# Metaformer kernel on one core: products stored by image, half of the masks on GpSimd, and the front in smaller pieces

## The chip, the core and the metric

The kernel runs on one core of a Trainium2 chip. The metric is the device time of one execution in microseconds, as the median of several runs. TensorE (PE) multiplies and transposes, VectorE (DVE) and ScalarE (ACT) read what it leaves in PSUM, GpSimd (POOL) works between buffers in SBUF, and SyncE (SP) issues most DMAs. Each engine goes through its own instructions in order and waits for the others by semaphores.

## What is computed

A block of four parts, each a norm and a mixing step with a residual: a spectral convolution, experts, a swept convolution, experts.

```python
# x (8, 32, 64, 64); _ln_c: mean and variance over the 32 channels of a pixel
def _L0_conv_ref(x, w1_real, w1_imag, w2_real, w2_imag):
    xf = jnp.fft.rfft2(x, norm='forward')
    top = jnp.einsum('bixy,ioxy->boxy', xf[:, :, :32, :32], w1)
    bot = jnp.einsum('bixy,ioxy->boxy', xf[:, :, -32:, :32], w2)
    ...
    return jnp.fft.irfft2(out_fft, s=(h, w), norm='forward')

def _L0_ffn_ref(x, gate_w, gate_b, weight1, weight2):      # L1 the same
    logits = jnp.einsum('bsd,ed->bse', x, gate_w) + gate_b  # 16 experts
    probs = jax.nn.softmax(logits, axis=1)                  # over the 4096 tokens
    vals, idx = jax.lax.top_k(probs.transpose(0, 2, 1), K)  # K = 8
    ...
    pooled = jnp.einsum('bked,bke->bed', gathered, topv)
    h = jax.nn.gelu(jnp.einsum('ebd,edh->ebh', h, weight1), approximate=False)
    out = jnp.einsum('ebh,eho->ebo', h, weight2)
    weighted = jnp.einsum('beo,bke->bkeo', out, topv)
    return outputs.at[arange(B)[:, None], flat_idx].add(weighted)

# L1_conv: four sweeps (down, up, right, left); each row is
#   row + relu(conv1d of the row before, 9 taps)

x = x + _L0_conv_ref(_ln_c(x), ...)
t = _to_tokens(x); t = t + _L0_ffn_ref(_ln_t(t), ...)
x = _from_tokens(t, x); x = x + _L1_conv_ref(_ln_c(x), ...)
t = _to_tokens(x); t = t + _L1_ffn_ref(_ln_t(t), ...)
```

## The kernel before

The whole problem stays in SBUF: RA, RB, RC and RD (the last two together RCD) hold 128 x 8192 floats each, RE the spectral weights and scratch. Partitions are four images times 32 channels, or, after a transposition, pixels. PS is PSUM, eight banks of 512 floats. There is no scheduler: each engine's program is written out by hand, and the order on an engine is that of the code.

**First norm** (`norm_tokens(0)`, L477, L801, L999): x comes in eight pieces of 1,024 columns on SP's queue, the six tables `dft` in one load on ACT's. TensorE first runs 42 multiplications of nothing (`keep_warm`), then `centre_group(g)` (L459) subtracts the channel mean of group g into a PSUM slot of two banks; ACT squares it (L809), VectorE sums (L966), ACT takes the root (L791), VectorE the reciprocal (L973) and scales (L976), TensorE applies the transform along a row as the `follower` (L496), ACT drains it into RC (L798). There are four slots, so group g+4 is centred once group g's follower is drained. VectorE takes total(g+1) ahead of norm(g).

**Spectrum** (from L501): `turn_rows_of_spectrum(j)` transposes a group (L430), ACT or VectorE drains it into RA, `spectrum(c)` (L537) transforms along the columns for chunk c of eight, `spread` (L1041, L840) copies the result into the block form XB in eight pieces each on VectorE and ACT, and `mix(c)` (L557) multiplies by the weights, 64 matmuls that the profile counts as 128, in four parts k of a bank each. VectorE drains parts 0 and 1 into Z, ACT parts 2 and 3. Groups 4 to 7 are turned at the head of mix(0) to mix(3). The weights of chunk c (2 MB, `wspec`) go into one of three places; chunks 3 to 7 are asked for by SP when mix(c-3), the last user of the place, is done (L360). Ahead of mix(0) stand the two projections of the gates and 14 idle multiplications.

**Back** (L572 to L641): the products are transposed (two times eight groups), ACT copies the imaginary part to `imtmp` (L856), VectorE combines both into V (L1062, L1063), chunk by chunk. V lies in RA as (chunk, x, a, re/im, y and image), so that the 128 numbers that `turn_spectrum` (L596, L430) takes for one image stand eight floats apart. ACT drains (L861), `dft_h` (L603) and `dft_w_back` (L633) invert the transform, with transpositions between them.

**Experts** (`experts(l)`): logits by token, the eight largest of each row by `max`, and `match_replace` (L1119) into L2 with the eight replaced by -3e38, while ACT forms all exponentials E (L885). `mask(g)` (L1126) on VectorE keeps E where L2 was replaced, for four quarters g. TensorE turns quarter g (L430), 14 idle multiplications follow for g < 2, VectorE scales (`weigh`, L1132), and `pool_tokens` (L686) sums. `rs_row` and `rs_rep` carry the reciprocal of the softmax's sum by ACT, TensorE (L702) and ACT. In the second layer VectorE takes the four masks in a row, in the first the last two stand between the weighings.

The swept convolution (L753 to L779 and its partners) is not touched.

## Time and profile before

| what | us |
|---|---|
| median of 3 runs | 574.76 (574.59 to 575.63) |
| the profiled execution | 575.6 |
| its span | 573.8 |
| TensorE busy | 533.4 |
| VectorE, ACT, GpSimd busy | 333.3, 296.9, 63.6 |
| granted clock, mean | 0.976 |

The span is what the trace covers; 1.8 us of the profiled execution lie around it. The trace gives for each engine when an instruction started, how long it took and what ended its wait. Neighbouring instructions of one line are merged into one row with a count. TensorE's matmuls overlap, so that the row of a group is more telling than the time of one.

### The profile page before, as it was taken

What the parts mean: (1) busy time and instruction counts of PE and PEld (TensorE: products, weight loads), DVE (VectorE), ACT (ScalarE), POOL (GpSimd) and SP (SyncE); (2) the same over time, 40 slices, a digit from 0 to 9 for tenths busy, and PEclk for the clock granted to TensorE, in tenths of its full rate; (3) what the DMA queues carried; (4) which work ended last, traced back from release to release, by engine and by line L of the source; (5) the groups of instructions that cost most, each with busy time, mean ns of one, the idle gap of its engine ahead of it and who ended that gap; (6) DMA issues with size and microseconds to landing.
All of it is one profiled execution on the core that took longest, in us unless ns stands there. A gap on an engine that the chain in (4) does not pass through costs nothing.

```text
span 573.8 us, 26756 instructions
## 1 busy us (share of the span) xinstructions
PE 533.4 (93%) x11432; PEld 494.5 (86%) x11432; DVE 333.3 (58%) x826; ACT 296.9 (52%) x762; POOL 63.6 (11%) x62
## 2 busy tenths in 40 slices
PE   8889899899997999899999999989999999977895
PEld 8889899899996895689999999989999999976782
DVE  2767686635459926874445444434544455389826
ACT  4556575732278502465555555576666555567300
POOL 4000000020021000000000033320000044640000
PEclk9999999999999888999999999999999999999978
DMA  9941782330000000000000024330000244410007
GB/s 353 376 149 55 270 336 83 137 159 2 1 2 0 2 22 0 2 1 3 2 0 0 4 61 103 76 39 3 0 0 2 47 76 70 78 29 1 2 3 292
DMA packets 48159, 40.80 MB, mean 71 GB/s; under 512 B 42554, under 2 KB 42810, under 8 KB 46877
## 3 DMA queue, kind: packets, MB, share of 16 engines
q1 hardware_dynamic: 46606, 37.27, 20.2%
q0 software_dynamic: 1344, 2.17, 1.8%
q8 instruction: 55, 0.90, 0.6%
q10 hardware_dynamic: 144, 0.39, 0.2%
q14 instruction: 10, 0.07, 0.0%
HBM read 27.49 MB, written 4.19 MB: 55 GB/s over the span
## 4 chain that ended last, share of the span: by engine, by line
PE 70%; DVE 18%; ACT 3%; SPq 2%; POOL 2%; issue 2%; DMA 1%; DVEq 0%; ACTq 0%
PE PS L769 34%; PE PS L557 6%; PE PS L469 4%; PE PS L430 4%; PE PS L603 3%; PE PS L686 3%; PE PS L633 3%; PE PS L762 3%; DVE sums L1084 2%; PE PS L537 2%; DVE RCD L1096 2%; PE PS L463 2%; PE PS L496 2%; DVE sums L966 2%; SPq L332 2%
## 5 line engine op out<-in xcount | busy, mean ns | idle before, releaser
L769 PE MATMUL PS<-RE,conv_sb 128*64 128x64 f32 x6048 | 228.7, 227 | 2.5 <-DVE RE L1198 2.0
L769 PEld LDWEIGHTS PS<-RE,conv_sb 128*64 128x64 f32 x6048 | 211.0, 137 | 11.7 <-DVE RE L1198 4.4
L1198 DVE SCALAR_TENSOR_TENSOR RE<-PS,RE 128x64 f32<-128x64 f32 x504 | 113.1, 225 | 120.9 <-PE PS L769 110.3
L762 PE MATMUL PS<-ones_bf,biasT 128*64 128x64 bf16 x1008 | 100.5, 192 | 0.5 <-DVE RE L1191 0.4
L902 ACT ACTIVATE RE<-RCD 128x128 f32 (+1 forms) x126 | 38.9, 310 | 52.1 <-DVE RE L1198 52.0
L762 PEld LDWEIGHTS PS<-ones_bf,biasT 128*64 128x64 bf16 x1008 | 60.0, 112 | 1.5 <-ACT RCD L798 0.5
L469 PE MATMUL PS<-warm 128*128 128x128 bf16 x524 | 39.1, 241 | 4.0 <-DVE ones_bf L961 1.5
L469 PEld LDWEIGHTS PS<-warm 128*128 128x128 bf16 x524 | 35.3, 109 | 5.4 <-ACT RB L882 1.6
L321 POOL DMA_DIRECT2D RE<-RCD x32 | 18.6, 588 | 181.7 <-ACT RCD L905 181.7
L902 ACT ACTIVATE RE<-RE 128x128 f32 (+1 forms) x63 | 26.6, 422 | 19.5 <-DVE RE L1198 17.2
L905 ACT COPY RB<-RE 128x128 f32 (+1 forms) x126 | 35.6, 283 | 1.5 <-DVE RE L1198 1.5
L557 PE MATMUL PS<-RE,RB 128*64 128x64 f32 x1024 | 32.4, 223 | 3.2 <-issue 3.2
L905 ACT COPY RCD<-RE 128x128 f32 (+1 forms) x122 | 34.4, 282 | 0.7 <-DVE RE L1198 0.7
L557 PEld LDWEIGHTS PS<-RE,RB 128*64 128x64 f32 x1024 | 31.0, 138 | 4.2 <-issue 3.6
L902 ACT ACTIVATE RE<-RB 128x128 f32 (+1 forms) x63 | 19.5, 310 | 25.2 <-DVE RE L1198 25.1
L966 DVE TENSOR_REDUCE sums<-RE 128x32 f32<-128x1024 f32 x16 | 19.4, 1217 | 20.0 <-ACT RE L809 20.0
L1041 DVE COPY RB<-PS 32x256 f32<-32x256 f32 x64 | 26.7, 417 | 7.2 <-PE PS L537 6.5
L861 ACT COPY RB<-PS 128x512 f32<-128x512 f32 (+1 forms) x24 | 16.2, 735 | 26.9 <-PE PS L430 26.9
L1084 DVE TENSOR_REDUCE sums<-RE 128x32 f32<-128x1024 f32 x16 | 19.4, 1212 | 16.4 <-ACT RE L873 9.4
L809 ACT ACTIVATE RE<-PS 128x1024 f32<-128x1024 f32 x16 | 16.2, 1020 | 24.4 <-PE PS L463 21.3
L339 POOL TENSOR_TENSOR RA<-RCD 128x1024 f32<-128x1024 f32 x6 | 17.2, 2894 | 103.9 <-DMA RCD<-RB 103.9
L840 ACT COPY RB<-PS 32x256 f32<-32x256 f32 x64 | 24.1, 377 | 8.4 <-PE PS L537 7.7
(120 smaller groups left out, 753.0 us busy)
## 6 DMA issues: line engine op xcount, KB each, us to landing
RE<-wspec SPq DMA_DIRECT2D x8, 2048.0 KB, 9.0
RA<-x_in SPq DMA_DIRECT2D x8, 512.0 KB, 7.4
RCD<-x_in SPq DMA_DIRECT2D x1, 4096.0 KB, 13.2
out<-RA SPq DMA_DIRECT2D x8, 512.0 KB, 3.5
RCD<-RB SPq DMA_DIRECT2D x48, 64.0 KB, 2.1
RCD<-RB SPq DMA_DIRECT2D x26, 32.0 KB, 1.9
conv_sb<-conv_w SPq DMA_DIRECT2D x1, 768.0 KB, 20.0
RE<-RCD SPq DMA_DIRECT2D x8, 96.0 KB, 4.1
```

The source lines that it names most:

```text
L430: m = pe.transpose(out, lhs[own], ident[own, own])
L469: pe.matmul(PS[:, bank, 0:P], warm[:, :], warm[:, :], start=True, stop=True)
L557: m = pe.matmul(o[:, x % 2, y], XB[:, c % 2, x, 2 * y + a].rearrange("p r q b -> p (r q b)"), WR[:, c % 3, a, x, y, :], start=True, stop=True)
L762: pe.matmul(conv_bank(u, h)[MO * o:MO * (o + 1)], biasT[:, s, MO * o:MO * (o + 1)], ones_bf[:, :], start=True, stop=False)
L769: m = pe.matmul(conv_bank(u, h)[MO * o:MO * (o + 1)], conv_sb[:, s, d, MO * o:MO * (o + 1)], prev, start=False, stop=(d == 2))
L840: m = act.copy(o, i)
L902: act.activation(rowb[:, u], row_at(SRC[s], s, q, u), ACT.Identity).then_inc(s_row, 1)
L905: act.copy(row_at(DST[s], s, q, u), state[:, state_slot(s, u), :, 1:1 + HO]).then_inc(s_arc, 1)
L966: dve.tensor_reduce(sums[:, 32 * g:32 * g + 32], square[:, g % 2, 0:1024].rearrange("p (a c) -> p a c", c=C), AX_X, ALU.add).then_inc(s_su ...
L1041: m = dve.tensor_copy(o, i)
L1084: dve.tensor_reduce(sums[:, 32 * g:32 * g + 32], square[:, g % 2, 0:1024].rearrange("p (a c) -> p a c", c=C), AX_X, ALU.add).then_inc(s_su ...
L1198: dve.scalar_tensor_tensor(out=state[:, state_slot(s, u), k, 1:1 + HO], in0=conv_bank(u, h), scalar=0.0, in1=rowb[:, u, k], op0=ALU.max, o ...
```

## The change

Four things change.

1. *Front.* Piece 0 of x is loaded in two halves. ACT's queue loads the centring table alone, the other five come on SP's queue behind piece 1. 24 idle multiplications stand first, where 42 stood. ACT's first activation is a Sqrt of one column.
2. *Norm's tail and first chunk.* Group 0 is turned ahead of follower(6). The drain of the last follower and that of turned group 2 are cut in two, half on ACT and half on VectorE. spread(0) runs in two halves of eight copies each per engine; mix(0) starts its parts 0 and 1 on the first half and turns group 4 between parts 1 and 2.
3. *Products by image.* V is stored as (chunk, re/im, image, y, q), `imtmp` in the same order, and the table `inv_h` is permuted to fit. ACT and VectorE now read PSUM with eight floats between neighbours and write in a row, and TensorE reads the 128 numbers of an image in a row.
4. *Masks.* Quarters 2 and 3 are formed otherwise: ACT takes Exp of L2 in place (zero where replaced) ahead of `rs_row`, and GpSimd subtracts that from E.

```diff
 @block.sync
-            for g in range(8):
+            sp.dma_start(RA[:, 0:BANK], x_in[:, 0:BANK]).then_inc(s_x[0], 16)
+            sp.dma_start(RA[:, BANK:2 * BANK], x_in[:, BANK:2 * BANK]).then_inc(s_xh, 16)
+            for g in range(1, 8):
                 sp.dma_start(RA[:, 1024 * g:1024 * g + 1024], ...).then_inc(s_x[g], 16)
+                if g == 1:
+                    sp.dma_start(dft_sb[:, 1:6, :], dft[:, 1:6, :]).then_inc(s_dft, 16)
 @block.gpsimd
+            def masks(l):
+                for g in (2, 3):
+                    pool.wait_ge(s_exl, 2 * l + g - 1)
+                    chosen = CW[l][:, 1024 * g:1024 * g + 1024]
+                    pool.tensor_tensor(run_rows(chosen) if l else chosen, part(E, l, g), part(L2, l, g),
+                                       ALU.subtract).then_inc(s_mskp, 1)
...
             pool.memset(state, 0.0).then_inc(s_pad, 1)
+            masks(0)
...
             squares(1)
+            masks(1)
 @block.tensor
                 for n in range(8):                     # centre_group(0, g)
+                        if g == 0 and n == Q:
+                            pe.wait_ge(s_xh, 16)
...
+                    if ln == 0 and g == 6:             # norm_tokens
+                        pe.wait_ge(s_fd, 5)
+                        turn_rows_of_spectrum(0)
                     follower(g)
...
-            keep_warm(7, 42)
-            pe.wait_ge(s_dft, 16)
+            keep_warm(7, 24)
+            pe.wait_ge(s_ctr, 16)
             def dft_w(g):
+                if g == 0:
+                    pe.wait_ge(s_dft, 16)
...
-            pe.wait_ge(s_fd, 5)
-            turn_rows_of_spectrum(0)
             pe.wait_ge(s_fd, 6)
             turn_rows_of_spectrum(1)
             pe.wait_ge(s_fd, 8)
+            pe.wait_ge(s_fdd, 1)
             turn_rows_of_spectrum(2)
             turn_rows_of_spectrum(3)
...
                     wait_rows_turned(pe, 2)            # spectrum(0)
+                    pe.wait_ge(s_t2d, 1)
...
             def mix(c):
-                pe.wait_ge(s_xbd, c + 1)
-                pe.wait_ge(s_xba, c + 1)
-                if c < 4:
-                    turn_rows_of_spectrum(4 + c)
+                if c == 0:
+                    pe.wait_ge(s_mixh, 1)
+                    pe.wait_ge(s_mixd, 1)
+                else:                                  # as before
...
-                    elif k >= 2:
+                    elif k == 2:
+                        pe.wait_ge(s_xbd, 1)
+                        pe.wait_ge(s_xba, 1)
+                        turn_rows_of_spectrum(4)
                         pe.wait_ge(s_gpc, 1)
...
-                turn(c, [V_of_b[:, c, :, BH * bl + bh] for bh in range(BH) for bl in range(BL)])
+                turn(c, [V_of_b[:, c, BH * bl + bh] for bh in range(BH) for bl in range(BL)])
...
-                    pe.wait_ge(s_msk, 4 * l + g + 1)
+                    if g < 2:
+                        pe.wait_ge(s_msk, 2 * l + g + 1)
+                    else:
+                        pe.wait_ge(s_mskp, 2 * l + g - 1)
 @block.scalar
-            act.dma_start(dft_sb[:], dft).then_inc(s_dft, 16)
+            act.dma_start(centre, dft[:, 0, :]).then_inc(s_ctr, 16)
...
+                        if ln == 0 and g == 7:         # drain_follower
+                            o, i = o[..., 0:8], i[..., 0:8]
...
             act.wait_ge(s_set, N_SET)
+            act.activation(std[:, 255:256], eps_sb[:, 0:1], ACT.Sqrt, bias=eps_sb[:, 0:1], scale=1.0 / C)
             norm_tokens(0, f1_pairs)
-            drain(2, t1_pairs)
+            act.wait_ge(s_full, 3)
+            for o, i in t1_pairs(2):
+                act.copy(o[:, :, 0], i[:, :, 0]).then_inc(s_da, 1)
...
-                for o, i in xb_pairs(c, 2):            # spread(c); the same on VectorE
+                if c == 0:
+                    for o, i in xb_pairs(c, 2, 0, X8 // 2):
+                        m = act.copy(o, i)
+                    m.then_inc(s_mixh, 1)
+                for o, i in xb_pairs(c, 2, 0 if c else X8 // 2):
...
-                act.copy(imtmp[:, c % 2, :], banks(4 * (c % 2) + 2, 2)).then_inc(s_tmp, 1)
+                im = banks(4 * (c % 2) + 2, 2).rearrange("p (y r q b) -> p r b y q", r=2, q=Q, b=B)
+                act.copy(im_of(c), im).then_inc(s_tmp, 1)
...
+                act.wait_ge(s_rep, l + 1)
+                for g in (2, 3):
+                    left = part(L2, l, g)
+                    act.activation(left, left, ACT.Exp, bias=negmax[:, :]).then_inc(s_exl, 1)
                 act.wait_ge(s_rt, l + 1)
 @block.vector
-            for j in (0, 1, 3):
-                drain(j, t1_pairs)
+            drain(0, t1_pairs)
+            dve.wait_ge(s_ff, 8)
+            for o, i in f1_pairs(7, ln_slot(7)):
+                dve.tensor_copy(o[..., 8:16], i[..., 8:16]).then_inc(s_fdd, 1)
+            drain(1, t1_pairs)
+            dve.wait_ge(s_full, 3)
+            for o, i in t1_pairs(2):
+                dve.tensor_copy(o[:, :, 1], i[:, :, 1]).then_inc(s_t2d, 1)
+            drain(3, t1_pairs)
...
-                by_re = banks(4 * (c % 2), 2).rearrange("p (a x r n) -> p x a r n", x=X8, a=2, r=2)
-                by_im = imtmp[:, c % 2, :].rearrange("p (a x r n) -> p x a r n", x=X8, a=2, r=2)
+                by_re = banks(4 * (c % 2), 2).rearrange("p (y r q b) -> p r b y q", r=2, q=Q, b=B)
+                by_im = im_of(c)
...
-                mask(0)
-                mask(1)
-                if l == 1:
-                    mask(2)
-                    mask(3)
+                for g in range(2):
+                    mask(dve, l, g, s_msk)
                 weigh(0)
-                if l == 0:
-                    mask(2)
                 weigh(1)
-                if l == 0:
-                    mask(3)
                 weigh(2)
                 weigh(3)
```

The line numbers of the changed program differ: L489 is the centring (L459 before), L536 the follower (L496), L458 the transposition (L430), L499 the idle multiplication (L469), L572 the spectrum (L537), L599 the products (L557), L552 the gates (L518). TensorE from the centring of group 7 to mix(0), before:

```order
10 L459 MATMUL PS<-dft_sb,RA 128x128 x8
11 L496 MATMUL PS<-dft_sb,RCD 128x128 x24
12 L430 MATMUL PS<-dft_sb,RCD 128x64 x64
13 L469 MATMUL PS<-warm 128x128 x16
14 L537 MATMUL PS<-dft_sb,RA 128x128 x16
15 L518 MATMUL PS<-gate_sb,dft_sb 128x64 x2
16 L469 MATMUL PS<-warm 128x128 x14
17 L430 MATMUL PS<-dft_sb,RCD 128x64 x16
18 L557 MATMUL PS<-RE,RB 64x2x32 x64
```

The same stretch of TensorE in the changed program:

```order
10 L489 MATMUL PS<-dft_sb,RA 128x128 x8
11 L536 MATMUL PS<-dft_sb,RCD 128x128 x8
12 L458 MATMUL PS<-dft_sb,RCD 128x64 x16
13 L536 MATMUL PS<-dft_sb,RCD 128x128 x16
14 L458 MATMUL PS<-dft_sb,RCD 128x64 x48
15 L499 MATMUL PS<-warm 128x128 x16
16 L572 MATMUL PS<-dft_sb,RA 128x128 x16
17 L552 MATMUL PS<-gate_sb,dft_sb 128x64 x2
18 L499 MATMUL PS<-warm 128x128 x14
19 L599 MATMUL PS<-RE,RB 64x2x32 x32
20 L458 MATMUL PS<-dft_sb,RCD 128x64 x16
21 L599 MATMUL PS<-RE,RB 64x2x32 x32
```

Sixteen transpositions (group 0) moved ahead of the last two followers, and group 4's moved into the middle of mix(0).

VectorE in the first expert layer, from the replacement on, before:

```order
94 L1119 MATCH_REPLACE RCD<-top,RB 128x4096
95 L1121 RECIPROCAL rsum<-expsum 128x1
96 L1126 SCALAR_TENSOR_TENSOR RCD<-RCD 128x1024 x2
97 L1132 TENSOR_TENSOR RE<-PS,rstd 128x1024
98 L1126 SCALAR_TENSOR_TENSOR RCD<-RCD 128x1024
99 L1132 TENSOR_TENSOR RE<-PS,rstd 128x1024
100 L1126 SCALAR_TENSOR_TENSOR RCD<-RCD 128x1024
101 L1132 TENSOR_TENSOR RE<-PS,rstd 128x1024 x2
```

VectorE there in the changed program, the same rows up to the pooled sums:

```order
99 L1188 MATCH_REPLACE RCD<-top,RB 128x4096
100 L1190 RECIPROCAL rsum<-expsum 128x1
101 L354 SCALAR_TENSOR_TENSOR RCD<-RCD 128x1024 x2
102 L1194 TENSOR_TENSOR RE<-PS,rstd 128x1024 x4
103 L1211 TENSOR_TENSOR pooled<-PS,rs_rep 32x16 x8
```

Two masks are left on VectorE, with the four weighings behind them; the second layer reads the same (it had four masks in a row, then four weighings).

ACT in the second expert layer, from the loading of the exponential's table on, before:

```order
266 L885 ACT_TABLE_LOAD
267 L885 ACTIVATE RCD,expsum<-RCD,negmax 128x4096
268 L887 COPY rs_row<-PS 1x128
269 L889 COPY rs_rep<-PS 32x128
270 L891 ACT_TABLE_LOAD
```

ACT there in the changed program:

```order
269 L940 ACT_TABLE_LOAD
270 L940 ACTIVATE RCD,expsum<-RCD,negmax 128x4096
271 L944 ACTIVATE RCD<-RCD,negmax 128x64x16 x2
272 L946 COPY rs_row<-PS 1x128
273 L948 COPY rs_rep<-PS 32x128
274 L950 ACT_TABLE_LOAD
```

Two exponentials of a quarter stand between the large one and the copy of the row `rs_row`; GpSimd has two subtractions of 128x1024 per layer, the last of its work in the second.

## Rows read from the trace of the kernel before

**Rows 1.** The page: engines, busy us (share of the span) xinstructions.

```profile
PE 533.4 (93%) x11432; PEld 494.5 (86%) x11432; DVE 333.3 (58%) x826; ACT 296.9 (52%) x762; POOL 63.6 (11%) x62
```

**Rows 2.** Timeline 0 to 18: start us, us, engine, line, operation, xcount [idle before <-releaser].

```profile
1.52 4.66 PE L469 MATMUL PS<-warm 128*128 128x128 bf16 x42 [1.52 <-DVE ones_bf L961]
...
5.97 7.83 PE L459 MATMUL PS<-dft_sb,RA 128*128 128x128 f32 x64
...
8.53 1.28 ACT L809 ACT_TABLE_LOAD   x1 [8.53 <-PE PS L459]
...
11.78 1.28 ACT L791 ACT_TABLE_LOAD   x1
...
13.82 1.23 DVE L976 TENSOR_TENSOR RCD<-PS,rstd 128x1024 f32<-128x1024 f32 x1
```

**Rows 3.** Stretches: us, busy (and count) of PE, PEld, DVE, ACT, POOL; clock, DMA.

```profile
6.00:7.00 1.00, 1.00 (x7) 1.00 (x6) 0.00 (x0) 0.00 (x0) 1.00 (x1) 1.00 1.02 418
7.00:8.00 1.00, 1.00 (x11) 1.00 (x11) 0.00 (x0) 0.00 (x0) 0.66 (x1) 1.00 1.00 406
```

**Rows 4.** Timeline, TensorE at the end of the first norm.

```profile
36.77 3.84 PE L496 MATMUL PS<-dft_sb,RCD 128*128 128x128 f32 x32 [1.52 <-DVE RCD L976]
```

**Rows 5.** Timeline, spread(0), idle multiplications, the gate copy, first products.

```profile
45.81 3.07 ACT L840 COPY RB<-PS 32x256 f32<-32x256 f32 x8 [2.33 <-PE PS L537]
45.81 3.43 DVE L1041 COPY RB<-PS 32x256 f32<-32x256 f32 x8 [1.03 <-PE PS L537]
...
47.79 0.94 PE L469 MATMUL PS<-warm 128*128 128x128 bf16 x14
...
49.27 0.29 DVE L1046 COPY proj<-PS 128x128 f32<-128x128 f32 x1
...
49.94 3.95 PE L557 MATMUL PS<-RE,RB 128*64 128x64 f32 x128
```

**Rows 6.** Timeline: a weights' load issued, and TensorE's pauses without a releaser.

```profile
53.93 15.86 SPq L360 DMA_DIRECT2D RE<-wspec  x3
...
62.58 0.33 PE L557 MATMUL PS<-RE,RB 128*64 128x64 f32 x2 [2.19 <-issue]
...
81.92 2.05 PE L537 MATMUL PS<-dft_sb,RA 128*128 128x128 f32 x16
...
91.39 7.51 PE L557 MATMUL PS<-RE,RB 128*64 128x64 f32 x250 [0.65 <-issue]
```

**Rows 7.** Waits: engine, line waited for: us in total, times, longest us.

```profile
PE PS L557 <- issue: 3.2, 3, 2.2
```

**Rows 8.** Timeline: combining (L1062), turning V (RA) and an image (RCD), a strided drain.

```profile
106.91 0.69 DVE L1062 TENSOR_TENSOR RA<-PS,RE 128x512 f32<-128x512 f32 x1
...
117.12 1.23 DVE L1068 COPY RCD<-PS 128x1024 f32<-128x1024 f32 x1 [6.43 <-PE PS L603]
118.80 1.98 PE L430 MATMUL PS<-dft_sb,RA 64*128 64x64 f32 x32
...
133.74 1.22 PE L430 MATMUL PS<-dft_sb,RCD 64*128 64x64 f32 x32
```

**Rows 9.** Timeline, second expert layer, and the first one's first pooling.

```profile
529.72 3.71 ACT L885 ACTIVATE RCD<-RCD,negmax 128x4096 f32<-128x4096 f32 x1 [1.27 <-DVE negmax L1118]
...
534.12 4.63 DVE L1126 SCALAR_TENSOR_TENSOR RCD<-RCD 128x1024 f32<-128x1024 f32 x4
...
538.46 0.40 PE L702 MATMUL PS<-rs_row,ones 1*32 1x128 f32 x2
...
539.94 2.06 PE L686 MATMUL PS<-RE,RB 128*64 128x32 f32 x64 [1.08 <-DVE RE L1132]
198.88 2.06 PE L686 MATMUL PS<-RE,RA 128*64 128x32 f32 x64
```

**Rows 10.** Timeline: GpSimd's square and VectorE's scaling at one time.

```profile
169.00 1.89 POOL L393 TENSOR_TENSOR RE<-RA 128x1024 f32<-128x1024 f32 x1 [3.56 <-ACT RA L875]
169.11 2.33 DVE L1096 TENSOR_TENSOR RCD<-RCD,rstd 128x512 f32<-128x512 f32 x1
```

49 lines of the change are left out of this document (31 added, 18 removed).

## The prediction

> **What bounds the kernel now.** The page's shares come first: TensorE is busy 93% of the span, VectorE and ACT little over half [rows 1]. So the chain of work mostly follows TensorE, and an edit pays where TensorE stands idle, or where its own instructions get shorter. The timeline then shows what ends its waits. At the start it runs idle multiplications until 5.97, then centres, and the first scaled group is late because ACT loads two tables one after the other [rows 2]. At the norm's end it waits 1.52 us for a scaling [rows 4]. Ahead of the first products it waits for the spread, which is a matter of VectorE's eight copies [rows 5]. In the products it pauses at 60.4 to 62.6 with nothing that releases it, and again at 91.39 [rows 6]. Behind the products VectorE sets the pace, and the transpositions of V take longer than others of their shape [rows 8]. In the second expert layer it waits 1.08 us for a weighing that stands behind four masks [rows 9].
>
> **The front.** The 42 idle multiplications take 4.66 us, 111 ns each [rows 2]; 24 end at 1.52 + 24 x 0.111 = 4.2. Both loads had to be there at 5.97 before, 896 KB in all; 320 KB are enough now for the first half group. I take them as landed by 4.2, with 5.2 as the bound. The clock column says 1.00, but TensorE did 7 matmuls in the seventh microsecond and 11 in the eighth [rows 3]: it ran at the lower level until about 7. Group 0's end (8.46, ACT starts at 8.53) contains 0.97 us at about 225 ns a matmul. Starting at 4.15 it has 2.8 us of that, 12.5 matmuls, and 3.5 at 112 ns: it ends at 7.3, group 1 at 9.1 where it ended at 10.3. That is **1.15 us**, not the 1.8 us of the start, since the saved time is slow time.
>
> ACT's table load of 1.28 us at 8.53 and that at 11.78 go; one stands in the idle time ahead of group 0 [rows 2]. Between the tables ACT made two squares (9.81 to 11.78, 1.0 each); a pass of VectorE over a group costs 1.23 as the scaling does; and from the second table's end at 13.06 to the scaling at 13.82 root and reciprocal took 0.76, of which the reciprocal, about half, is left behind VectorE's second sum. From group 1's end (9.1): 1.0 + 1.23 + 0.4, so the first scaling starts at 11.8, 2.7 behind it. Before it was 13.82 - 10.3 = 3.5 behind. **0.85 us**. What follows (sum, scaling, follower, drain, next centring) is the same ring as before and only shifts.
>
> At the end of the norm group 0's 16 transpositions (0.6, half of the 1.22 that 32 took [rows 8]) fit into the 1.52 us of waiting [rows 4], and are gone from behind follower 7. Against this the turning of groups 2 and 3 waits for the half drains, about 0.1 to 0.15 more than group 1's turning covers. With half of group 2's drain on VectorE (behind two full drains) ending just under the 16 idle multiplications, it makes **0.45 us**. Together the front gives 2.45.
>
> **First products.** A copy of 32x256 costs 0.43 (3.43 for eight) on VectorE and 0.38 on ACT [rows 5]; one of 128 numbers a row costs 0.29 by the gate copy. So the first halves end 2.4 us after spectrum(0), well ahead of the end of the idle multiplications (48.73, 2.95 behind spectrum(0), whose spread starts at 45.81), and mix(0) starts then instead of at 49.94 less group 4's turning of 0.6. But 16 copies take 4.4 us on ACT, at 0.27 each by the same ratio, where eight took 3.1, then comes group 4's drain, which itself now waits for TensorE's middle of mix(0), then spread(1). I find spread(1) done 9.75 us behind spectrum(0), and TensorE there at 9.45; before it was there at 10.05. Of the 0.65 gained at the end of mix(0), **0.25** is left at mix(1).
>
> **The pauses.** In the order of the program I counted instructions, two for each pass of a matmul and one for each separate wait. There are three pauses, 3.2 us in all [rows 7]; those in mix(1), mix(5) and mix(6) stand exactly 1,024 and 256 instructions apart and nothing releases them: TensorE waits for code. The first ended 8.65 us after the weights' load behind it was issued (53.93 to 62.58), the last 9.5 us after mix(4)'s end at 81.92, when the last load goes out [rows 6]: code that is asked for behind such a load comes with its end. In the changed program the boundaries lie at other places: at the end of spectrum(3), in mix(2) after 217 of 256 instructions, in mix(5) and mix(6). Counted from mix(0)'s end, the first is reached at 8.6 (code at 8.8: 0.2). There the next block is asked for, 1.9 us behind the load issued at 6.9; it comes at 15.6 to 16.4 and is wanted at 13.0, a new pause of about 3. The two late ones stay at 0.2 and 0.7. Sum 4.1 against 3.2: **-0.9 us**. Bounds: all of it gone, +3.2, or 1.5 worse.
>
> The Trainium skill, page "Runtime: NRT & Kernel Launch", section "Instruction fetch mechanics", says that the code comes in blocks of 16 KiB with 256 instructions and that the cost of a boundary is mostly hidden. The distances agree, the pause of 2.19 us does not; by that sentence this term would be +3.2 and the sum 8.3.
>
> **Products by image.** 32 transpositions of V take 1.98 us, 32 of an image 1.22 [rows 8]: 0.7 to 0.8 per pair of groups. V's numbers now stand in a row. For the later two pairs I take 0.7 each. For the first two the ACT drains gate: the third group starts when the first is drained, so half a pair less ahead of it and a shorter last group make 0.85. **2.25 us**. The combination itself is VectorE's pace, sixteen operations of 0.69, and must not get longer. It now reads PSUM eight floats apart. The nearest row is a drain that reads 128 floats apart in 1.23 for 1,024 numbers [rows 8], which is what the scaling pays that reads in a row [rows 2]; so I take zero, with half speed (0.5 more each) as the other bound.
>
> **Masks.** Second layer: VectorE's four masks (4.63, 1.14 each) put the first weighing at 538.67 and pooling at 539.94. With two, the weighing ends at 537.6, and TensorE is next bound by its own row: the spread of rs_row at 538.46 and 0.40 [rows 9]. Pooling starts at 538.86: **1.1 us**. An exponential of 4,096 numbers costs 3.71, a copy of 256 costs 0.38 [rows 5], so one of a quarter 1.05, or 1.15 with the bias; two from 534.1 on put rs_row's copy at 536.4 to 536.7, still ahead of 538.46. GpSimd's two subtractions at 1.89 each (its square [rows 10]) end by 540.2, wanted at 540.8 and 543.4. In the first layer TensorE is busy up to the pooling at 198.88 with its own rows: zero.
>
> Here a wait can replace the removed one. VectorE's scaling of 512 numbers took 2.33, where 512 cost 0.69 otherwise [rows 8], when GpSimd's square had started 0.11 us earlier [rows 10]: two operations that both read two SBUF buffers don't run together, and the first holds on. The second mask and GpSimd's first subtraction are such a pair, and start within a tenth of each other: the mask at 534.12 + 1.14 = 535.26, the subtraction behind the exponential at 534.12 + 1.05 to 1.15 + 0.1 for the semaphore, 535.27 to 535.37. I take the mask as first.
>
> The page "SBUF — State Buffer" of the Trainium skill, section "Who interferes with whom", has it as an exclusive lock of the pair of ports that both engines share. The trace agrees, and by this rule the change could lose on what it moves to GpSimd; rival 1 has the price.
>
> **Sum.** 2.45 + 0.25 - 0.9 + 2.25 + 1.1 = 5.15. The profiled execution took 575.6 with 1.8 outside the span; it would be 570.45. It lies 0.84 above the median, which makes the forecast 574.76 - 5.15 = **569.6 us**.
>
> **Rivals.**
> 1. GpSimd first: the mask ends 1.1 behind the subtraction's end, 538.3; VectorE's weighing and TensorE's turning follow, pooling at 540.2, a loss of 0.2 where 1.1 was to be gained, and 0.6 in the first layer. 569.6 + 1.9 = 571.5. For it: the two starts are a tenth apart. Against: by these prices the mask is ahead by a hair. 18%.
> 2. The code arrives in time: the new pause in mix(2) doesn't come. 566.6. For it: a request just ahead of the load would be served at once. 15%.
> 3. The clock stays at its lower level over the first two groups, since fewer idle multiplications run ahead or a load is late: 32 matmuls at 225 ns end at 11.4 instead of 9.1. 571.9. 12%.
> 4. Slower: VectorE's combination pays for eight floats' distance. 16 operations at half speed give +8.5: 578.1. It decides from 0.32 us more on each (0.69 to 1.01). Against it stands the strided drain at full price; that has one input, this has two. 4%.
>
> **How the numbers follow.** The main case has 47%, the rivals 49, and 4 are left for the change doing less than it says (front or V without effect, 572 to 574.5). The range takes in rivals 1 to 3: 566.4 to 572.2. A measurement of this kernel tells about 0.2% (1.15 us). Faster by more: all but rival 4 and half of the rest, 0.93; within 0.03; slower 0.04.
>
> **What would show it.** First squares at 7.4 and no table load behind; first scaling at 11.8; no wait for the scaling above 1.0 at the norm's end; first products 3.0 behind spectrum(0); a pause of 3 in mix(2) with about 108 of its 128 matmuls done; DVE combinations still 0.69; 32 transpositions of V in 1.2 to 1.3; second mask 1.22 long in both layers, pooling at the spread of rs_row. A second mask above 2, a combination above 1.0, or group 1's centring ending after 10.3 would make the forecast wrong.

## The result, and the profile after

| | us |
|---|---|
| kernel before, median of 4 runs | 575.19 (574.59 to 575.8) |
| changed kernel, median of 4 runs | 566.37 (564.2 to 566.58) |
| ratio | 0.9838, 95% interval 0.9811 to 0.9865 |
| profiled execution of the changed kernel, and its span | 566.56, 564.7 |

Faster by 8.8 us, where the prediction said 5.15 less than 574.76 and gave 566.4 as its lower end. The result lies 0.03 us below that end. The two profiled executions differ by 9.0 us. I cut both traces at the same instructions. A stretch runs from the start of one named piece of work to the start of the next:

| stretch | before | after | difference | predicted |
|---|---|---|---|---|
| start to spectrum(0) | 43.77 | 41.16 | -2.61 | -2.45 |
| spectrum(0) to the last matmul of the products | 54.90 | 56.44 | +1.54 | +0.65 |
| from there over the combination to the experts' first exponential (L940) | 90.46 | 87.12 | -3.34 | -2.25 |
| expert layer 0 and second norm, to the first row of the sweeps | 70.41 | 70.37 | 0.0 | 0 |
| four sweeps | 234.25 | 231.14 | **-3.11** | 0 |
| to the exponential of layer 1, and on to pooling | 46.14 | 45.00 | -1.14 | -1.1 |
| pooling to the end | 33.84 | 33.52 | -0.3 | 0 |

The largest surprise is the sweeps, which no edit touches. Two others stand in the second and the third row, in opposite directions.

**Front.** The timeline of the changed kernel, 0 to 18 us, answers [rows 2]. The first row of its centring is groups 0 and 1, and the next two groups waited 0.35 us for x; there is one table load, at 1.18, and the first scaling starts at 11.45 instead of 13.82.

```profile
1.18 1.28 ACT L876 ACT_TABLE_LOAD   x1 [1.18 <-PEq L1325]
...
1.52 2.74 PE L499 MATMUL PS<-warm 128*128 128x128 bf16 x24 [1.52 <-DVE ones_bf L1020]
...
4.12 4.72 PE L489 MATMUL PS<-dft_sb,RA 128*128 128x128 f32 x32
...
9.19 3.84 PE L489 MATMUL PS<-dft_sb,RA 128*128 128x128 f32 x32 [0.35 <-DMA RA<-x_in]
...
11.45 1.22 DVE L1035 TENSOR_TENSOR RCD<-PS,rstd 128x1024 f32<-128x1024 f32 x1
```

TensorE from the norm's end on, answering [rows 4] and [rows 5]. The scaling is waited for 0.88 us, not 1.52, and a group is turned ahead of it (0.71 at 32.81). The first products start 4.9 us behind spectrum(0), where it was 6.17; the second ones wait 0.31 for ScalarE's spread, as the prediction had it.

```profile
32.81 0.71 PE L458 MATMUL PS<-dft_sb,RCD 64*128 64x64 f32 x16
...
34.40 3.84 PE L536 MATMUL PS<-dft_sb,RCD 128*128 128x128 f32 x32 [0.88 <-DVE RCD L1035]
...
41.16 3.79 PE L572 MATMUL PS<-dft_sb,RA 128*128 128x128 f32 x32
...
53.10 0.72 PE L458 MATMUL PS<-dft_sb,RCD 64*128 64x64 f32 x16 [0.31 <-ACT RB L894]
```

**Pauses.** TensorE in the products, answering [rows 6], [rows 7]. The pauses stand where they were forecast: at the end of spectrum(3) (after 13 of 16), in mix(2) after 108 of 128 matmuls, and in mix(6). They have 0.92, 1.93 and 0.53 us, 3.4 together; forecast were 0.2, 3, 0.7, and 0.2 in mix(5) that didn't come. But the 16 matmuls of spectrum(4) behind the long pause take 3.68 us, where the sixteen of spectrum(5) take 2.05: TensorE's granted clock was at its lower level, half of the full one, from 67.4 to 70.8.

```profile
60.26 0.49 PE L572 MATMUL PS<-dft_sb,RA 128*128 128x128 f32 x3 [0.92 <-issue]
...
61.32 3.37 PE L599 MATMUL PS<-RE,RB 128*64 128x64 f32 x108
66.63 0.80 PE L599 MATMUL PS<-RE,RB 128*64 128x64 f32 x20 [1.93 <-issue]
67.36 3.68 PE L572 MATMUL PS<-dft_sb,RA 128*128 128x128 f32 x16
...
75.49 2.05 PE L572 MATMUL PS<-dft_sb,RA 128*128 128x128 f32 x16
...
90.78 7.04 PE L599 MATMUL PS<-RE,RB 128*64 128x64 f32 x234 [0.53 <-issue]
```

**Products by image**, answering [rows 8]. VectorE's combination stays at 0.69, and 32 turnings of V take 1.22, as those of an image do, where they took 1.98.

```profile
107.11 0.69 DVE L1132 TENSOR_TENSOR RA<-PS,RE 128x512 f32<-128x512 f32 x1
...
115.91 1.22 PE L458 MATMUL PS<-dft_sb,RA 64*128 64x64 f32 x32
```

**Masks**, layer 1, answering [rows 9]. VectorE makes two masks, 1.22 each (2.36 for both): neither is held up. GpSimd's subtractions take 3.35 and 2.35, not 1.89. The first runs beside VectorE's second mask (527.70 to 528.92) and is 1.0 us longer than the second, in both layers and in every trace with these masks. So the wait between the two engines that the prediction read from [rows 10] seems to be there again, this time on GpSimd; it is read from the overlap alone, as no run moves the two apart. The subtractions end at 531.13 and 533.43, over 2 us ahead of the turnings that read them (533.22 and 535.85). Pooling starts right behind TensorE's own row at 530.90.

```profile
526.55 2.36 DVE L354 SCALAR_TENSOR_TENSOR RCD<-RCD 128x1024 f32<-128x1024 f32 x2
...
527.78 3.35 POOL L418 TENSOR_TENSOR RCD<-RCD 128x1024 f32<-128x1024 f32 x1 [20.64 <-ACT RCD L944]
...
530.90 0.40 PE L747 MATMUL PS<-rs_row,ones 1*32 1x128 f32 x2
531.07 2.36 POOL L418 TENSOR_TENSOR RCD<-RCD 128x1024 f32<-128x1024 f32 x1
...
531.23 2.06 PE L728 MATMUL PS<-RE,RB 128*64 128x32 f32 x64
```

### The profile page after: what moved, and what is told of

Read it like the earlier page. It is cut to its first block, busy times and chain, and to the rows that moved or that the text cites. A ratio compares the mean times of both kernels' runs of the same rounds, so it can differ in the third digit from the quotient of the medians.

```text
span 564.7 us, 26747 instructions
## 1 busy us (share of the span) xinstructions
PE 528.3 (94%) x11414; PEld 490.2 (87%) x11414; DVE 331.9 (59%) x832; ACT 300.7 (53%) x774; POOL 75.1 (13%) x66
## 4 chain that ended last, share of the span: by engine, by line
PE 71%; DVE 17%; ACT 4%; POOL 3%; issue 2%; SPq 2%; DMA 1%; DVEq 0%; ACTq 0%
PE PS L814 35%; PE PS L599 5%; PE PS L499 4%; PE PS L458 3%; PE PS L675 3%; PE PS L728 3%; PE PS L572 3%; PE PS L807 3%; PE PS L645 3%; DVE sums L1153 2%; DVE RCD L1165 2%; DVE sums L1025 2%; PE PS L493 2%; PE PS L489 2%; PE PS L536 2%
## 5 line engine op out<-in xcount | busy, mean ns | idle before, releaser
L814 PE MATMUL PS<-RE,conv_sb 128*64 128x64 f32 x6048 | 227.8, 227 | 0.7 <-DVE RE L1253 0.7
L814 PEld LDWEIGHTS PS<-RE,conv_sb 128*64 128x64 f32 x6048 | 211.1, 137 | 8.7 <-DVE RE L1253 0.9
L1253 DVE SCALAR_TENSOR_TENSOR RE<-PS,RE 128x64 f32<-128x64 f32 x504 | 113.4, 225 | 117.3 <-PE PS L814 109.4
L499 PE MATMUL PS<-warm 128*128 128x128 bf16 x506 | 37.1, 238 | 4.0 <-DVE ones_bf L1020 1.5
L499 PEld LDWEIGHTS PS<-warm 128*128 128x128 bf16 x506 | 33.4, 108 | 5.4 <-ACT RB L937 1.6
L599 PE MATMUL PS<-RE,RB 128*64 128x64 f32 x1024 | 32.2, 223 | 2.5 <-issue 2.5
L599 PEld LDWEIGHTS PS<-RE,RB 128*64 128x64 f32 x1024 | 30.8, 138 | 3.5 <-issue 2.7
L458 PE MATMUL PS<-dft_sb,RCD 64*128 64x64 f32 x640 | 26.2, 227 | 2.1 <-DVE RCD L354 0.9
L1111 DVE COPY RB<-PS 32x256 f32<-32x256 f32 (+1 forms) x64 | 25.6, 400 | 4.2 <-PE PS L572 3.4
```

The costliest lines, as they stand in the source:

```text
L458: m = pe.transpose(out, lhs[own], ident[own, own])
L499: pe.matmul(PS[:, bank, 0:P], warm[:, :], warm[:, :], start=True, stop=True)
L599: m = pe.matmul(o[:, x % 2, y], XB[:, c % 2, x, 2 * y + a].rearrange("p r q b -> p (r q b)"), WR[:, c % 3, a, x, y, :], start=True, stop=True)
L814: m = pe.matmul(conv_bank(u, h)[MO * o:MO * (o + 1)], conv_sb[:, s, d, MO * o:MO * (o + 1)], prev, start=False, stop=(d == 2))
L1111: m = dve.tensor_copy(o, i)
L1253: dve.scalar_tensor_tensor(out=state[:, state_slot(s, u), k, 1:1 + HO], in0=conv_bank(u, h), scalar=0.0, in1=rowb[:, u, k], op0=ALU.max, o ...
```

## Where the sweeps' three microseconds came from

A sweep is 63 rows one behind the other: TensorE, then VectorE (L1198 before, L1253 after) in two halves, L769 and L814 being TensorE's matmuls. Before, the four took 56.55, 58.39, 58.05 and 56.75 us from first to last row; after, 56.55, 56.61, 56.67 and 56.66. Two of them were slow, for two different reasons.

*The second sweep.* VectorE goes through its rows in a loop of four. In the second sweep of the kernel before, each first row of a turn starts late. Its timeline at such a place (330.80), VectorE alone:

```profile
329.75 0.23 DVE L1198 SCALAR_TENSOR_TENSOR RE<-PS,RE 128x64 f32<-128x64 f32 x1 [0.26 <-PE PS L769]
330.16 0.22 DVE L1198 SCALAR_TENSOR_TENSOR RE<-PS,RE 128x64 f32<-128x64 f32 x1 [0.18 <-PE PS L769]
330.80 0.48 DVE L1198 SCALAR_TENSOR_TENSOR RE<-PS,RE 128x64 f32<-128x64 f32 x2 [0.41 <-PE PS L769]
```

The changed kernel:

```profile
325.85 0.22 DVE L1253 SCALAR_TENSOR_TENSOR RE<-PS,RE 128x64 f32<-128x64 f32 x1 [0.27 <-PE PS L814]
326.25 0.23 DVE L1253 SCALAR_TENSOR_TENSOR RE<-PS,RE 128x64 f32<-128x64 f32 x1 [0.17 <-PE PS L814]
326.74 0.23 DVE L1253 SCALAR_TENSOR_TENSOR RE<-PS,RE 128x64 f32<-128x64 f32 x1 [0.27 <-PE PS L814]
```

The profile names TensorE as releaser, but the two halves then follow each other without a gap (x2), so both were ready. The trace also records the branch at the loop's end. From its end to VectorE's next instruction it took 134 ns in all loops but this one, where it took 263. Fourteen times 0.13 is 1.8 us. I suspected the place of the loop in VectorE's program: it starts at instruction 314 in the kernel before, and at 322 in the changed one. (The count is of the program as it is built, from 0, with the jumps into the loops, which the trace doesn't record.)

*The third sweep.* Before, TensorE waits 1.39 us in its third row, for VectorE, which waits for ScalarE, which waits for moved rows. The kernel before:

```profile
378.40 0.36 DVE L1198 SCALAR_TENSOR_TENSOR RE<-PS,RE 128x64 f32<-128x64 f32 x2 [1.84 <-ACT RE L902]
...
381.31 0.41 ACT L902 ACTIVATE RE<-RE 128x128 f32<-128x128 f32 x1 [1.97 <-DMA RE<-RCD]
...
381.75 0.36 DVE L1198 SCALAR_TENSOR_TENSOR RE<-PS,RE 128x64 f32<-128x64 f32 x2 [1.83 <-ACT RE L902]
...
382.03 0.57 PE L769 MATMUL PS<-RE,conv_sb 128*64 128x64 f32 x12 [1.39 <-DVE RE L1198]
```

The trace's DMA records show why. All of the moved rows' packets on SyncE's queue but the last 17 are through by 379.2; those start at 379.90. In between, from 379.02 to 379.90, a packet of 16 KB passes, of the queue that carries TensorE's instructions. In the changed kernel that packet comes 0.5 us after the last row packet. What shifted it is again a count: TensorE's program is 32 instructions shorter there.

## The experiments

Labels with b_ are edits of the kernel before, labels with a_ are edits of the changed kernel. All 18 kernels ran beside the kernel before on their chip, and a ratio is to that. Other chips than the first gave medians of 573.3 to 574.2 us for the kernel before, against 575.19 on the first, so that two edits of the changed kernel on different chips can't be told apart by their times to better than about 2 us. b_ref, a_warm42, a_nosqrt, a_whole, a_notail and a_xwhole have one execution each, the profiled one: their total time says little, and they are read by stages.

### Code positions in the sweeps

**b_align.** On the kernel before:

```diff
+                        for _ in range(16):
+                            dve.wait_ge(s_pad, 1)
                         dve.wait_ge(s_pad, 1)
...
-            keep_warm(0, 20)
+            keep_warm(0, 12)
...
-                    keep_warm(7, 36)
+                    keep_warm(7, 28)
```

The waits are met long before, and two of them make one instruction of VectorE.

> The kernel before with VectorE's program 8 instructions longer ahead of the sweeps (16 extra waits that are already met) and TensorE's 32 matmul instructions shorter ahead of the third sweep (two warm-ups of 8 products less), which gives both engines the code positions that the changed kernel has in the sweeps; nothing that is computed changes. Theory 1 (code position): VectorE's branch at the end of each turn of the loop of the second sweep, 264 ns before, falls to 134 ns and the sweep from 58.4 to 56.6 us; the 1.4 us wait in row 3 of the third sweep goes, that sweep falls from 58.1 to 56.7; in all 3.2 us, 572.0 us. Rival 2 (the sweeps gained from what runs beside them at another time, not from code): both sweeps stay at 58.4 and 58.1, 575.2 us. Rival 3 (only VectorE's part is code, the third sweep's wait is chance): 573.4 us.

**b_dve16.** The same loop with `range(32)`, and nothing on TensorE.

> The kernel before with VectorE's program 16 instructions longer ahead of the sweeps (32 extra waits that are already met), nothing else. Theory 1a (the place that the second sweep's loop crosses comes once in as many instructions as a 16 KB piece of code holds): no loop crosses it now, the second sweep falls to 56.6 us, the third keeps its 1.4 us wait, 573.4 us. Rival 1b (such a place comes every 64 instructions): the third sweep's loop crosses the next one, its branch goes to 264 ns and it grows by 1.8 us, so the second sweep's gain is given back, 575.2 us. Rival 2 (not code): no branch changes, 575.2 us.

**a_misalign.** On the changed kernel: `range(32)`, `keep_warm(0, 28)`, `keep_warm(7, 44)`.

> The changed kernel with the code positions put back to bad ones: VectorE's program 16 instructions longer ahead of the sweeps (met waits), so that the loop of the first sweep lies across the place that the second sweep's loop crossed in the kernel before, and TensorE's 32 matmul instructions longer ahead of the third sweep (two warm-ups of 8 products more), its position in the kernel before. Theory 1 (code position): the branches of the first sweep take 264 ns in place of 134 and it grows from 56.55 to 58.4 us; in the third sweep the last packet of the moved rows stands behind a 16 KB piece of code and the wait of 1.4 us in row 3 is back (58.1 us); 3.2 us in all, 569.6 us against 566.4. Rival 2 (not code position): the sweeps stay at 56.6 us each, 566.4 us.

**b_ref** and **a_ref** are the kernels before and after as they are, for a second trace of each.

> The kernel before as it is, for a second trace of it. Theory 1 (its slow sweeps and its pauses are the program's own): the sweeps take 56.6, 58.4, 58.1 and 56.7 us again and TensorE's pauses in the products 2.8 to 3.2 us in three. Rival 2 (the third sweep's wait is chance): it takes 56.7 us.

> The changed kernel as it is, on the same chip as the next one. Theory 1 (the sweeps' gain belongs to the program's code positions, the rest to the edits): its trace shows 56.6 us for each sweep, spectrum(0) at 41.2 and 30.1 us from the last combination's start back to the first drain of the experts as before, whatever chip it runs on; 566.4 us. Rival 2 (the sweeps' gain was chance of one execution): one of the two sweeps is above 57.5 us, 568 to 570 us. Beside it: where TensorE's clock falls is not set by the program, so the dip of 3.4 us in the products (67.4 us) may be absent, and the products then end 1.1 us earlier.

b_ref's pauses in the products are 2.8 us together, in two places and not three. The sweeps from first to last row, the start of VectorE's loop in each, and the two readings. The branch's time is the median of the 14 or 15 of a sweep; "code packet" is when TensorE's 16 KB packet starts, from the third sweep's first row.

| kernel | loop starts at | branch ns | sweeps us | code packet |
|---|---|---|---|---|
| before | 281, **314**, 352, 385 | 134, **263**, 134, 134 | 56.6, **58.4**, **58.1**, 56.8 | 0.62 |
| b_ref | the same | 134, **263**, 134, 134 | 56.5, **58.4**, **58.0**, 56.6 | 0.59 |
| b_image | the same | 135, **263**, 134, 134 | 56.5, **58.4**, **58.1**, 56.6 | 0.59 |
| b_align | 289, 322, 360, 393 | all 134 | 56.5, 56.9, 56.7, 56.6 | 1.32 |
| b_dve16 | 297, 330, 368, 401 | all 134 or less | 56.5, 56.6, **58.0**, 56.7 | 0.63 |
| a_misalign | **305**, 338, 376, 409 | **263**, 134, 134, 134 | **58.2**, 56.8, **57.7**, 56.6 | 0.46 |
| after, a_ref | 289, 322, 360, 393 | all 134 or 135 | 56.5, 56.6 to 56.7, 56.7, 56.6 | 1.31, 1.16 |
| a_warm42 (below) | the same as after | | 56.7, 56.7, **57.9**, 56.6 | 0.57 |
| a_whole (below) | 281, **314**, 352, 385 | 134, **263**, 134, 134 | 56.6, **58.4**, 56.6, 56.7 | 1.28 |

Both effects can be put in and taken out by instructions that compute nothing. A loop of 22 instructions is slow when it starts at 305 or 314, and fast at 297 or less and from 322 on. So there is one place, ahead of an instruction from 319 to 322, which costs 0.13 us a turn when the loop lies across it. In b_dve16 the third loop lies at 368 to 389 and is fast, so such a place doesn't come every 64 instructions: rival 1b falls. No instruction packet but TensorE's passes in the kernel before from 321.13 to 373.48, in which nearly all turns of that loop lie, so its body isn't loaded anew at each turn. What the place is stays open. So do 0.3 us that the second sweep of b_align keeps with all its branches at 134 ns. The Trainium skill, page "Runtime: NRT & Kernel Launch", section "Instruction fetch mechanics", says that a taken branch whose target lies outside the two 16 KiB pages that are held forces a load. The trace doesn't show that here: 129 ns and no packet is something smaller, which that section doesn't tell.

For the third sweep, the packet at 0.46 to 0.63 us goes with a slow one, at 1.16 and later with a fast one, and this holds in all 20 traces. a_warm42, made for another question, has 36 TensorE instructions more than the changed kernel and brought the wait back (waits of all engines at that handover, 371 to 377 us):

```profile
ACT RE L961 <- DMA RE<-RCD: 2.2, 2, 1.8
PE PS L814 <- DVE RE L1253: 2.1, 2, 1.3
```

In whole executions: b_align 571.7 us, ratio 0.9975 (0.9949 to 1.0002), which is 1.4 us where 3.2 were expected; b_dve16 572.32, 0.9973 (0.9957 to 0.9989), 1.5 of 1.8; a_misalign 571.04 (0.9951, 0.9921 to 0.9981), against 566.37 and 566.7 of the changed kernel on two other chips (a_ref's ratio is 0.986, 0.9785 to 0.9935), 4.5 us more where 3.2 were expected. In its trace the sweeps have 2.9 of that, and 1.5 stand between the exponential of layer 1 and pooling, where the clock fell (see a_masks_dve). b_align was short, and its interval ends at 2.9, so it ran again:

**b_align5.**

> The run b_align again (the kernel before with the changed kernel's code positions in the sweeps), with more rounds. Theory 1: 3.2 us faster than before on the same chip, a ratio of 0.9944. Rival 2 (something else in the execution takes half of it back): 1.4 us faster again, 0.9975.

571.27 us, 0.9955 (0.993 to 0.9979): 2.6 us, with 3.2 inside the interval and 1.4 too. The sweeps themselves are 2.6 to 2.8 us shorter in both traces (231.42 and 231.45 against 234.25 and 234.05). What the medians lack of that stays open. The clock doesn't fill it in these traces: it is low for 3.4 us from 62.3 and 63.2 on, and the products take 56.1 and 56.4 us, against 54.9 and 55.1 in the two traces of the kernel before, which has the same code there; but its own drop at 111 to 113, worth 0.6 to 1.1 us (see b_image), is missing in them.

### Which edit moved the code

**a_whole.** The changed kernel, with spread(0) in one piece:

```diff
-                if c == 0:
-                    for o, i in xb_pairs(c, 0, 0, X8 // 2):
-                        m = dve.tensor_copy(o, i)
-                    m.then_inc(s_mixd, 1)
-                for o, i in xb_pairs(c, 0, 0 if c else X8 // 2):
+                for o, i in xb_pairs(c, 0):
```

and the same on ScalarE and in `mix`.

> The changed kernel with the spread of the first group in one piece, so that the first products wait for all of it, and rows group 4 are turned ahead of them, as before. Theory 1 (the prediction's term): the first products start 6.17 us behind spectrum(0) in place of 4.90, but the spread of group 1 bounds the second products, and the end of all products is at most 0.5 us later, measured from spectrum(0). Rival 2: the whole 1.27 us is on the path. Beside it, VectorE's program has 8 instructions less, all those that the changed kernel has more than before ahead of the sweeps: by the theory of code position the second sweep's branches take 264 ns again and it takes 58.4 us.

The first products came 6.17 us behind spectrum(0), as expected. At mix(1) the changed kernel is 0.1 us ahead of it (12.58 against 12.68 behind spectrum(0)). From spectrum(0) to the end of the products it took 54.32 us, less than a_ref's 55.20: the pause at the end of spectrum(3) shrank from 0.8 to 0.2 and that in mix(2) to 1.9. So the halves gain nothing there; what they win at mix(0) is waited away for code. And the second sweep took 58.4 us. The eight instructions by which VectorE's program grew are those of the halved spread. An edit meant for the 46th microsecond brought 1.8 us from the 320th on.

### Pauses

**a_halves.** The changed kernel, SyncE's loads of weights cut in two (and the count waited for in `mix` to fit):

```diff
-                sp.dma_start(RE[:, WCOLS * (c % 3):WCOLS * (c % 3 + 1)], wspec[c]).then_inc(s_wc[c % 3], 16)
+                for half in range(2):
+                    if c > 2 and half:
+                        sp.wait_ge(s_mix, 4 * (c - 2) + 2)
+                    w0, w1_ = WCOLS // 2 * half, WCOLS // 2 * (half + 1)
+                    sp.dma_start(RE[:, WCOLS * (c % 3) + w0:WCOLS * (c % 3) + w1_],
+                                 wspec[c][:, w0:w1_]).then_inc(s_wc[c % 3], 16)
```

> The changed kernel with the spectral weights of groups 2 to 7 loaded in two halves of 1 MB each, the second half from group 3 on issued half a group of products later. Theory 1 (TensorE's pauses in the products are its code, which is queued behind 2 MB loads that follow each other without a gap): the code comes within the gaps, the pauses of 3.4 us in spectrum(3), mix(2) and mix(6) shrink to under 1.5, 564.2 us. Rival 2 (the code's own latency makes them): the pauses stay within 0.5 us of 3.4, 566.4 us. Rival 3 (slower): a second half lands after its products want it, because its load starts 1.9 us later, and each group waits 0.3 us or more for weights, 568 us.

563.63 us (563.18 to 564.0), ratio 0.9835 (0.9783 to 0.9887). That is 2.7 and 3.1 us below the changed kernel on two other chips; the ratios to the kernel before (0.9838 and 0.986 for the changed kernel) don't tell them apart. The trace does: no wait of TensorE in the products is without a releaser any more. TensorE's waits from 40 to 100 us (waited for: us in total, times, longest), of a_ref:

```profile
PE PS L599 <- issue: 2.7, 3, 2.2
PE PS L572 <- issue: 0.8, 1, 0.8
PE PS L458 <- DVE RA L1133: 0.5, 1, 0.5
PE PS L458 <- ACT RB L894: 0.3, 1, 0.3
```

And of a_halves:

```profile
PE PS L463 <- DVE RA L1138: 0.5, 1, 0.5
PE PS L463 <- ACT RB L899: 0.3, 1, 0.3
PE PS L604 <- DVE RCD L1129: 0.3, 1, 0.3
```

From spectrum(0) to the products' end it takes 51.34 us, 3.9 less than in a_ref, and the clock doesn't fall there. Rival 3 would be a wait for weights of 0.3 us in each group; there is none. The records of the DMA queues agree: in the changed kernel TensorE's code packets start at 57.82 and 64.34, the second 1.1 us ahead of the end of the two loads that fill the queue from 51.8 to 65.46; in a_halves they start at 55.21 and 60.67. A pause ends 2.2 to 2.4 us behind the start of such a packet: 57.82 and 60.26, 64.34 and 66.63, 88.40 and 90.78 here, 60.23 and 62.58 in the kernel before. So it is the late start of the packet that makes the pause. And counted over the trace's records of TensorE, weight loads and waits included, each of the 53 pauses without a releaser that 18 of the 20 traces have here stands 1,473 records from the start or a multiple of 256 further.

**b_halves.** The same edit on the kernel before.

> The kernel before with the spectral weights of groups 2 to 7 loaded in halves as in the run a_halves, nothing else. Theory 1 (its pauses of 3.2 us are code queued behind 2 MB loads, too): the pauses fall under 1 us and from spectrum(0) to the last product it takes 52.2 us in place of 54.9; 2.7 us less in all. Rival 2 (the gain of a_halves came from where the changed kernel's code lies): under 0.8 us less.

Its pauses are gone as well, and the stretch takes 51.97 us, against 54.90 in before and 55.14 in b_ref: 2.9 to 3.2 less. The stretch from spectrum(0) to the end of the products (us; busy time and count of PE, PEld, DVE, ACT, POOL; clock, DMA share, GB/s) of b_ref:

```profile
43.16:98.30 55.14, 51.41 (x1237) 49.41 (x1234) 40.77 (x85) 34.73 (x81) 0.53 (x1) 1.00 0.53 193
```

And of b_halves:

```profile
42.83:94.80 51.97, 50.95 (x1237) 49.11 (x1234) 40.77 (x85) 34.77 (x81) 0.53 (x1) 1.00 0.58 205
```

The engines have the same work; TensorE's idle time falls from 3.7 to 1.0 us. Whole executions gave less: 572.53 us, 0.9982 (0.9961 to 1.0004), 1.0 us, with an interval from zero to 2.2. So the gain is shown for the stage in one trace of each, and not for the execution.

**b_both.** b_align and b_halves together: nothing of the change.

> The kernel before with the changed kernel's code positions in the sweeps and with the loads in halves: none of the changed kernel's edits. Theory 1: both gains stand beside each other, 6.2 us faster than before, a ratio of 0.989, about two thirds of what the whole change brought. Rival 2: 2.5 us faster, the sum of what the two gave in whole executions so far, 0.9956.

569.51 us, 0.9943 (0.9922 to 0.9963): 3.3 us by the ratio, 3.7 by the medians. The stages of its trace are where theory 1 wants them (products 52.2, with two pauses of 0.8 us together left; sweeps 56.6, 57.0, 56.6, 56.7), and its profiled execution, 568.44, lies 6.0 below b_ref's 574.45. But the interval rules 6.2 out for the median. b_ref's 574.45 is a long one for its kernel, whose 23 runs beside it had a median of 573.25, so part of the gap is that single profiled executions were compared. The rest I can't place, since only profiled executions have stages. One difference recurs: before and b_ref have no drop of the clock between 500 and 550 us, while b_align, b_align5, b_dve16 and b_both have one or two there, of 3.4 or 6.8 us. Up to the pooling of layer 1 it costs those kernels 0.2 us, so it doesn't fill the gap either.

### The other parts

**b_image.** The kernel before with part 3 of the change alone (its diff stands ahead).

> The kernel before with the products' layout by image alone. Theory 1 (the term of the prediction): the last drain of the products' part moves 2.25 us earlier, 572.9 us; the stretch at TensorE's lower clock at 112.8 to 116.2 us stays. Rival 2: with the V turnings closer together the clock does not fall there, another 1.0 us, 571.9 us. Rival 3 (the combination pays for its new distances): it grows from 0.69 us to over 1.2, and the gain is under 0.5 us, 574.7 us or more. The sweeps stay as they were in all three.

571.36 us, ratio 0.9949 (0.9922 to 0.9976), 2.9 us. From the combination's end to the experts' exponential it takes 75.11 us. In before it was 78.44, and 77.38 in b_align and b_dve16. Those two have the old layout, too, but no drop of the clock at 112.8 us. So the layout has 2.27 us, and the other 1.06 of before's 3.34 was that drop, which b_image didn't have and the changed kernel neither. In b_ref, where the drop came at 111.5, it cost 0.64. The turning of V in the timeline of b_dve16:

```profile
117.87 1.98 PE L430 MATMUL PS<-dft_sb,RA 64*128 64x64 f32 x32
```

And in that of b_image:

```profile
109.71 1.22 PE L434 MATMUL PS<-dft_sb,RA 64*128 64x64 f32 x32 [0.65 <-DVE RA L1068]
```

**a_masks_dve.** All masks on VectorE again.

> The changed kernel with all eight masks back on VectorE and without the two exponentials on ScalarE, so that the masks of GpSimd are the one part undone. Theory 1 (the term of the prediction): layer 0 does not change, pooling of layer 1 starts 1.1 us later, 567.5 us against 566.4. Rival 2: GpSimd's two subtractions at 2.8 us each hold back as much as VectorE's, no change, 566.4 us. Rival 3: GpSimd's work in layer 0 slowed VectorE's drains, and layer 0 gains 0.5 us by its absence, 567.0 us.

568.34 us, 0.9905 (0.9872 to 0.9938), 2.0 and 1.6 us more than the changed kernel on two other chips. From the exponential of layer 1 to pooling it takes 10.22 us, against 9.07: the 1.1 us. But a_ref has 9.74, a_misalign 10.54 and a_halves 10.56 there, with the change's masks: in these the clock was low in that stretch or just ahead of it, and TensorE is now what pooling waits for. b_image, which has the masks of before and a drop at the same place (532.8, 6.5 us behind the exponential; 6.3 in a_misalign, 6.5 in a_halves), has 10.55. The timeline of a_halves:

```profile
523.46 1.58 PE L504 MATMUL PS<-warm 128*128 128x128 bf16 x14
...
524.98 1.12 PE L463 MATMUL PS<-dft_sb,RCD 64*128 64x64 f32 x16
...
526.03 1.41 PE L504 MATMUL PS<-warm 128*128 128x128 bf16 x14
```

The 14 idle multiplications take 1.58 in place of 0.95, and the turning 1.12 in place of 0.71. The masks' gain is 1.1 us at the full clock and none when it falls there. In between stands a_ref: its clock was low from 516.8 to 523.6 and that of a_masks_dve from 516.5 to 523.3, both to 2.3 us behind the exponential, and the gain between these two is 0.5. In layer 0 it is 9.75 us to pooling and 8.97 for it in the changed kernel, a_ref and a_masks_dve alike, so GpSimd costs nothing there.

**a_warm42.** 42 idle multiplications in the changed kernel.

> The changed kernel with 42 idle products ahead of the first centring as before, in place of 24. Theory 1 (the start's term of the prediction comes from the shorter warm-up): the first centring starts at 5.7 to 6.0 us and spectrum(0) at 42.3, 1.15 us later than 41.16. Rival 2 (the smaller pieces of x and tables bring it, since group 1 waits for its x until 9.2 us in any case): the second group still starts at 9.2 to 9.4 us and spectrum(0) is at most 0.3 us later, 41.2 to 41.5. Beside it: TensorE's code is 36 instructions longer ahead of the products, so the long pause in mix(2) should stand after about 90 of its 128 products, not 108.

567.4 us. The centring starts at 5.32, but spectrum(0) at 41.43, the same as a_ref's 41.42. The first scaling is 0.3 to 0.6 us late (11.72), the second is not against a_ref (14.37): rival 2. How far one trace can be trusted here, others show. Eight traces have the changed kernel's front (the changed kernel, a_ref, a_halves, a_halves96, a_best, a_masks_dve, a_misalign, a_whole), and spectrum(0) starts at 40.70 to 41.78 in them, at 41.29 in the mean; x comes earlier or later, and a_ref's second pair of groups waited 1.19 us for it. In eight with the front of the kernel before it is 42.83 to 44.03, mean 43.38. So the whole front gained 2.1 us in the mean, and differences of single traces are good to about half a microsecond. For the pause I was wrong: none stands in mix(2). The long one, 2.27 us, is one place earlier, after 124 of mix(1)'s 128 matmuls, and the others are after 39 in mix(4) (0.21) and 4 in mix(6) (0.86). Each of these is where a count of 36 instructions more puts a boundary of 256; which boundary is waited at is decided by the loads, and the sum stays (3.3 us).

**a_nosqrt.** Without the early root.

> The changed kernel without the root that loads ScalarE's table at the start. Theory 1 (the prediction's term of 0.85 us for the table): the load stands ahead of the first root again, the first scaling starts at 12.3 us or later in place of 11.45, and spectrum(0) at 42.0 in place of 41.16. Rival 2 (slack ahead of the third group hides the load): spectrum(0) moves by less than 0.3 us.

568.11 us. Both loads are back, as the timeline shows, and the first scaling starts at 13.02, spectrum(0) at 42.73: 1.3 us behind a_ref and 1.4 behind the mean of the eight, not 0.85.

```profile
7.73 1.28 ACT L856 ACT_TABLE_LOAD   x1 [7.73 <-PE PS L489]
...
10.98 1.28 ACT L836 ACT_TABLE_LOAD   x1
13.02 1.23 DVE L1034 TENSOR_TENSOR RCD<-PS,rstd 128x1024 f32<-128x1024 f32 x1
```

**a_notail.** Group 0 turned behind the norm.

> The changed kernel with group 0 of the turned rows after the norm in place of within its tail. Theory 1 (the prediction's term of 0.45 us): spectrum(0) starts 0.4 to 0.5 us later, measured from the first scaling. Rival 2 (the drains of the turned rows bound it): under 0.15 us. Rival 3: the turning is 0.71 us long and all of it is on the path, 0.7 us.

566.29 us. spectrum(0) starts at 42.65, with the first scaling at 11.15: 31.50 us between them, against 29.71 in the changed kernel, 1.8 us more and above all three expectations. (a_ref has 30.30, since its second scaling was held up by x.) The cause is VectorE's queue: its drain of group 0 (1.22) stands ahead of its half of the last follower's drain, and group 0 is now turned just then. The half drain starts at 39.76 (L1091 in the timeline below), 5.67 us behind the start of the last two followers; in a_nosqrt, which turns group 0 ahead of them, it is 3.88. This kernel undoes one edit and lets another turn against it, so it is no price of the turning alone.

```profile
38.62 1.22 DVE L1084 COPY RA<-PS 128x1024 f32<-128x1024 f32 x1 [3.06 <-PE PS L458]
39.76 0.68 DVE L1091 COPY RCD<-PS 128x512 f32<-128x512 f32 x1
```

**a_xwhole.** The first group of x and the six tables in one load each.

> The changed kernel with the first group of x in one piece on SyncE's queue and all six tables in one piece on ScalarE's, as before; the shorter series of idle products, the early root and the turning in the tail stay. Theory 1 (the pieces bring the start's term): the first centring starts 1 us or more later than 4.1 us, the first scaling too, and spectrum(0) is at 42.3 or later against 41.4. Rival 2 (the terms overlap: the table's load alone held the first scaling): the first centring starts later but spectrum(0) stays within 0.3 us of 41.4.

568.73 us. In the timeline the centring starts at 5.68, its wait is for the tables, and spectrum(0) at 43.76, as late as in the kernel before (43.77), although the early root, the 24 idle multiplications and the turning in the tail are there.

```profile
5.68 9.34 PE L483 MATMUL PS<-dft_sb,RA 128*128 128x128 f32 x64 [1.42 <-DMA dft_sb<-dft]
```

### Two faster versions, and one that is not

**a_best.** a_halves, and in the expert layers:

```diff
-                keep_warm(0, 110)
+                keep_warm(0, 96)
...
-                    if g < 2:
-                        keep_warm(7, 14)
```

> The changed kernel with the halved loads of weights, and in both expert layers without the two series of 14 idle products between the turned masks and with 96 idle products in place of 110 ahead of them. Theory 1 (idle products stand in the way where the clock has fallen): from the exponentials to pooling takes 9.75 us in layer 0, of which 0.75 is the tail of the 110 and 1.4 the two series of 14, so pooling starts 7.6 us after them; in layer 1, 9.1 or 10.6 by the clock, it takes 7.7; against the halved loads alone 2 to 4 us less, 560.5 us. Rival 2 (the idle products hold the clock up): the clock falls in the pooling and expert products, which then take longer by as much, 563.6 us. Rival 3 (GpSimd's second subtraction becomes the bound): pooling starts early but its fourth part waits for it, and the gain is 0.5 us in each layer, 562.6 us. TensorE's code is 84 instructions shorter ahead of the sweeps, so a piece of code may land in one of the handovers, 1.4 us more in the third sweep.

569.19 us, the median of executions from the shortest of all kernels to the longest of those made from the changed one. Pooling does start early: 8.31 us behind the exponential in layer 0 and 8.42 in layer 1. But then, in the profiled execution, the clock stays down for 30.7 us in each layer. The stretches of pooling and of the expert products in layer 0 (columns as above, the clock is the third from the right), of a_best:

```profile
189.90:205.87 15.97, 15.97 (x288) 15.60 (x288) 3.24 (x3) 1.54 (x2) 2.99 (x2) 0.50 0.01 2
205.87:216.60 10.73, 10.73 (x146) 9.77 (x144) 2.19 (x10) 0.28 (x1) 0.00 (x0) 0.50 0.10 27
```

And of a_halves:

```profile
189.70:198.60 8.90, 8.90 (x287) 8.68 (x287) 2.54 (x3) 1.54 (x2) 1.50 (x1) 1.00 0.02 4
198.60:207.20 8.60, 8.06 (x149) 7.16 (x145) 2.19 (x10) 0.28 (x1) 0.00 (x0) 0.74 0.13 35
```

That is rival 2, at a price of 9 us for these stretches alone. The four executions took 579.89, 569.59, 568.79 and 560.39 us: one escaped it.

**a_halves96.** a_halves with 96 for 110 only.

> The kernel with halved loads and 96 idle products in place of 110 ahead of the masks in both layers; the two series of 14 stay. Theory 1: in layer 0 pooling starts 9.0 us after the exponentials in place of 9.75, because the idle products end before the first mask is there, layer 1 stays, and TensorE's clock does not stay low; 562.9 us. Rival 2: a gap of 1 us behind the idle products is enough to keep the clock low, as without the series of 14, and pooling and expert products take 7 us longer in a layer in some executions; 563.6 us or more.

563.07 us (561.44 to 563.48), 0.9825 (0.9788 to 0.9861). Pooling of layer 0 starts 9.16 us behind the exponential, 0.6 earlier, and the clock recovers as before. Its products still have two pauses, 0.94 and 0.29 us, and take 52.61: the halves cut the pauses and don't always end them. a_halves and a_halves96 are both below the kernel before, by their intervals, and below the times of the changed kernel (566.37 and 566.7), which ran on other chips; which of the two is faster can't be told.

## Why the prediction was wrong

It failed by what it left out. **The sweeps** had no term in the sum. The prediction found that TensorE's code has positions that cost, worked them out for the products, and stopped there; it didn't ask the same of VectorE's and TensorE's code further on, though the trace of before shows two sweeps that are 1.3 to 1.8 us longer than the others with the same work. That was visible, and 3.1 us of the 8.8 are there. With that term the sum would have been 8.3, and 566.5 the forecast. That both sweeps got faster is luck all the same: a_misalign, with 16 VectorE instructions and 32 of TensorE more, loses nearly all of it again.

*Front*, 2.45 predicted, 2.61 measured (2.1 in the mean of eight traces each): the sum was near and its parts were not. Up to the first scaling it is 2.37 where 1.15 + 0.85 were forecast; from there to spectrum(0) 29.71 us in place of 29.95, so that the tail's 0.45 is 0.24. The start's 1.15 us was derived from the shorter series of idle multiplications; a_warm42 shows that this is worth a few tenths at most, since the second pair of groups waits for x. It is the pieces of x and of the tables that bring it (a_xwhole, 2.3 us). The table's 0.85 is 1.3 (a_nosqrt). Undone one at a time, these two cost 3.6 us, more than the whole front gained, because each alone holds the first scaling back. How the saved time divides between them is not shown.

*First products*, 0.25 predicted: the step is right in its times (first products 4.9 behind spectrum(0), forecast 2.95 + 1.9; a wait for ScalarE's spread at mix(1)), but 0.1 is left of it at mix(1), and nothing at the end of the products (a_whole).

*Pauses*, -0.9 predicted, -0.2 measured (3.4 us against 3.2), or -0.3 in a_ref. Places right to the matmul; sizes 0.9, 1.9, 0.5 in place of 0.2, 3, 0.7. The mechanism, code that comes behind a load, is what a_halves and b_halves show. Most of the rest of that stretch's 1.54 us is the drop of the clock at 67.4. a_ref has the same code, pauses of 3.5 us (one of 0.27 in mix(4) among them) and no drop, and takes 1.2 us less there. So the drop isn't set by the program, and in the other direction before had one at 112.8 that helped "products by image" by 1.06 in the comparison of the two traces. The two happened to cancel. The side sum of 8.3 for pauses that are hidden is misadded, too: with +3.2 in place of -0.9 it is 9.25. In no trace with whole loads did they vanish.

*Products by image*, 2.25 predicted, 2.27 measured. The combination at 0.69 takes rival 4 away. *Masks*, 1.1 predicted, 1.14 measured in the profiled execution; the second mask went first and the subtraction was the longer one, so rival 1 fell by the tenth of a microsecond it hung on. The term's size depends on the clock, which the prediction didn't say. The subtraction was taken as 1.89 and takes 2.35, or 3.35 beside the mask; it didn't matter, as both end ahead of their use.

*Rivals.* Rival 2's time, 566.6, is the one measured, but not its mechanism: the pause in mix(2) came. Rival 3 fell too: the 32 matmuls from 4.12 took 4.72 us, and the second pair of groups waits for x. The range was too narrow for a whole program in which an untouched half can move; its lower end took in only what could happen in the stages that the diff names.

## What to carry to other kernels

Before costing an edit, compare stretches that do the same work in the trace of before: a sweep or a layer that is longer than its twin shows a cost that any change of the instruction count may remove or bring. To test for it, put instructions that compute nothing ahead of the loop and take idle ones away. A large load that follows another without a gap also holds up the engines' own code. Cutting it in halves spaced by the work took 2.5 to 3.9 us off that stage in five traces, where splitting the computation took off nothing; in whole executions 1.0 us of it was seen in the kernel before, within the noise. Undo parts one at a time only where they don't share a path or a queue.

## What the runs showed of the hardware

- A loop of 22 instructions on VectorE costs 0.13 us more a turn when it lies across one place of its program (ahead of instruction 319 to 322 here), and nothing at fourteen other positions.
- A 16 KB packet of TensorE's code takes 0.88 to 1.5 us, and the last packets of another transfer can stand behind it (in before from 379.02 to 379.90, the 17 packets from 379.90 on): 1.1 to 1.4 us in a wait that the profile puts down to that transfer.
- TensorE's clock falls at other places in executions of one program (at 67.4 in one trace of the changed kernel and not in the other), for 3.4 us; in 16 of the 20 traces it is low for 6.8 us from between 175 and 186 on and again 27 us later. At 67.4 TensorE had just paused for 1.93 us, but a_ref has a pause of 2.2 at the same place and no drop: of 15 traces with such a pause in the products, 5 have a drop within 1.1 us behind it. It costs 1.2 us there (56.44 against a_ref's 55.20).
- Idle multiplications hold the clock up and stand in the way at once. Two series of 14 cost 0.85 us on the path (pooling of layer 0 at 9.16 in a_halves96 and 8.31 in a_best), and without them the clock stayed low behind them in the profiled execution, which cost 9 us (pooling and expert products 26.7 us against 17.5); one execution of four escaped it.
- GpSimd's subtraction of 128x1024, both inputs in SBUF, took 3.35 us where it started 0.1 us behind a VectorE mask that reads two buffers of SBUF, and 2.35 as the next one, without a mask beside it; the mask took 1.22 with and without.
